# Transposes by upper and lower 64 rows into two PSUM banks, in a gated linear-attention and feed-forward kernel on one core

## The reference

```python
x = _layernorm(x + attn(x))     # attn(x) = x + y
x = _layernorm(x + ffn(x))
# attn: xn = layer_norm(x)*gamma+beta ; Q, K, V = xn @ W.T + b, 16 heads of 64 ; gate = silu(xn @ Wg.T + bg)
def step(h, qkv):
    h = alpha[None, :, :, None] * h + k[:, :, :, None] * v[:, :, None, :]
    o = jnp.einsum('bhi,bhij->bhj', q, h)
# y = (o * gate) @ WO.T + bO
# ffn: three cycles of out = out + coupling * twist(out), coupling from a four-layer net over out
#      (256, 128, 64, 1 wide, gelu, sigmoid) and from a small net over the mean of x
```

## Time and profile before

| | |
|---|---|
| median of 3 runs | 1892.21 us (1891.94 to 1892.32) |
| the profiled execution | 1892.58 us |
| its span | 1890.8 us |
| TensorE busy (matmuls) | 1824.6 us, 96% |
| VectorE, ScalarE, GpSimd busy | 56%, 37%, 17% |
| granted TensorE clock, mean | 0.985 of full speed |

### The profile page before, as it was taken

One profiled execution on the slowest core, in us unless ns is written; L12 is line 12 of the kernel. 1 busy time (PEld: TensorE's weight loads), 2 busy tenths in 40 slices (PEclk: granted clock), 3 DMA queues, 4 the chain that ended last, 5 costly groups with the idle time before them and its releaser, 6 DMA issues.

```text
span 1890.8 us, 43949 instructions
## 1 busy us (share of the span) xinstructions
PE 1824.6 (96%) x19120; PEld 1396.9 (74%) x19120; DVE 1062.4 (56%) x2214; ACT 699.9 (37%) x1282; POOL 312.9 (17%) x244
## 2 busy tenths in 40 slices
PE   5999999999899999999989999999989999999996
PEld 4888888863588888885368888888437888888732
DVE  7565555555745555554665645555565555555556
ACT  3323333344433333334433332323443333233344
POOL 4121211102212121110221112121022111212002
PEclk8999999999899999999989999999999999999998
DMA  4000000000100000000010000000001000000001
GB/s 161 2 13 2 13 2 12 2 1 1 56 2 13 2 12 2 12 2 1 0 57 2 13 2 13 2 13 2 1 1 57 2 13 2 13 2 2 2 0 45
DMA packets 22817, 26.11 MB, mean 14 GB/s; under 512 B 3169, under 2 KB 21473, under 8 KB 22625
## 3 DMA queue, kind: packets, MB, share of 16 engines
q1 hardware_dynamic: 20624, 19.09, 3.2%
q10 hardware_dynamic: 2000, 4.20, 0.6%
HBM read 14.90 MB, written 8.39 MB: 12 GB/s over the span
## 4 chain that ended last, share of the span: by engine, by line
PE 94%; DVE 3%; ACT 2%; POOL 1%; issue 0%; DMA 0%; ACTq 0%; DVEq 0%; SPq 0%
PE bank L848 39%; PE bank L923 12%; PE bank L1078 9%; PE bank L911 7%; PE bank L875 6%; PE bank L902 6%; PE bank L1095 4%; PE bank L892 3%; PE bank L884 3%; PE bank L1121 1%; PE bank L1108 1%; DVE stats L582 1%; PE bank L839 1%; DVE v_sb L816 1%; PE bank L934 1%; DVE x_nf L809 1%
## 5 line engine op out<-in xcount | busy, mean ns | idle before, releaser
L714 DVE TENSOR_TENSOR o_g<-bank,gate 128x512 f32<-128x512 f32 x128 | 88.6, 692 | 484.6 <-PE bank L911 484.6
L362 POOL TENSOR_TENSOR k_end<-k_sc,pows 128x512 f32<-128x512 f32 x128 | 134.9, 1054 | 1075.6 <-DVE k_sc L615 1075.6
L436 ACT ACTIVATE q_sb<-q_sb,pows 128x384 f32<-128x384 f32 (+2 forms) x384 | 167.3, 498 | 331.6 <-DVE q_sb L624 331.6
L454 ACT ACTIVATE h_bd<-h_seq,pows 64x256 f32<-64x256 f32 x256 | 129.9, 507 | 323.5 <-DVE h_seq L736 320.3
L923 PE MATMUL bank<-wo,o_g 128*128 128x256 f32 x1024 | 243.5, 380 | 0.8 <-DVE o_g L714 0.8
L923 PEld LDWEIGHTS bank<-wo,o_g 128*128 128x128 f32 x1024 | 192.7, 190 | 32.9 <-DVE o_g L714 1.0
L446 ACT ACTIVATE k_tok<-bank 128x512 f32<-128x512 f32 x128 | 76.5, 598 | 299.9 <-PE bank L884 299.9
L703 DVE COPY_PREDICATED att<-causal,bank 128x1024 f32<-128x1024 int32 x128 | 167.3, 1307 | 6.2 <-PE bank L875 5.4
L911 PE MATMUL bank<-att,v_sb 128*64 128x128 f32 x2048 | 140.1, 279 | 0.0
L902 PEld LDWEIGHTS bank<-q_sb,h_bd 128*128 128x128 f32 x1024 | 134.1, 191 | 7.4 <-ACT h_bd L454 0.2
L902 PE MATMUL bank<-q_sb,h_bd 128*128 128x128 f32 x1024 | 134.9, 275 | 0.0
(11 more groups left out here) (137 smaller groups left out, 3213.6 us busy)
## 6 DMA issues: line engine op xcount, KB each, us to landing
x_in<-in_x SPq DMA_DIRECT2D x16, 512.0 KB, 4.3
out_y<-q_sb SPq DMA_DIRECT2D x8, 512.0 KB, 2.8
out_y<-x_nf SPq DMA_DIRECT2D x8, 512.0 KB, 3.1
v_sb<-in_wq ACTq DMA_DIRECT2D x1, 1024.0 KB, 5.2
v_sb<-in_wk SPq DMA_DIRECT2D x1, 1024.0 KB, 9.0
x1t<-in_wg ACTq DMA_DIRECT2D x1, 1024.0 KB, 9.4
x1t<-in_wv ACTq DMA_DIRECT2D x1, 1024.0 KB, 13.5
wo<-in_wo ACTq DMA_DIRECT2D x1, 1024.0 KB, 17.4
```

Of the source, the lines that this page charges most:

```text
L362: nc.gpsimd.tensor_tensor(k_end[:].rearrange("p (a z) (b r) -> p a (z b) r", z=2, r=BL), k_sc[:].rearrange("p (a z) (b r) -> p a (z b) r", ...
L436: last = nc.scalar.activation(q_sb[:, p % 2, d].rearrange("p (a z) n -> p a (z n)", z=2)[:, :, reach], q_sb[:, p % 2, 0].rearrange("p (a z ...
L454: nc.scalar.activation(h_bd[rows, :, e * DH:(e + 1) * DH], h_seq[rows, :, :], ACT.Copy, scale=pows[rows, p, HP:HP + 1]).then_inc(s_hbd, 1)
```

## The change

Each 128 x 128 transpose becomes two of 64 rows by 128 columns. The upper 64 rows go into one bank and the lower 64 into the next, 64 columns each; what reads them picks the halves out of two banks. To have pairs of banks free, the bank plan of the attention changes: k and g always use bank 0, q bank 1, the updates bank 1, the transposed keys banks 0 and 1, the transposed input banks 2 and 3, and values go round banks 2 to 5. With this go changed waits on TensorE: the q projection waits for `s_hend`, the keys' transposes wait for the query and gate evacuations, and the transposes of the next step's input stand between g's projection and `y_part` at p = 6 instead of behind the keys. ScalarE scales the input's transposes ahead of `tokens_of` there.

```diff
-        def k_bank(p):
-            return p % 2
-        def q_bank(p):
-            return 1 - p % 2
         def g_bank(n):
-            return n % NP % 2 if n else 5
+            return 0 if n else 5
+        def halves_of(first_bank, first, count):
+            return psum[:, first_bank:first_bank + 2, first * DH:(first + count) * DH].rearrange(
+                "p r (c n) -> p c r n", n=DH)
+        def in_halves(rows):
+            return rows.rearrange("p (c r n) -> p c r n", r=2, n=DH)
...
         def final_rows(t, c):
-            return bank[(2, 0, 4, 6)[t] + c // 2][:, (c % 2) * D:(c % 2 + 1) * D]
+            first_bank = (2, 0, 4, 6)[t]
+            return psum[:, first_bank:first_bank + 2, c * P:(c + 1) * P]
         def v_bank(m):
-            return bank[(2, 3, 5, 1, 2, 3, 0, 5)[m]]
+            return bank[2 + m % 4]
...
-            def tokens_of(n, bk):
+            def tokens_of(n):
                 act.wait_ge(s_kt, n + 1 + C0)
                 act.wait_ge(s_upd, n + C0)
-                nc.scalar.activation(k_tok[:], part(bk, NC), ACT.Copy).then_inc(s_ktok, 1)
+                nc.scalar.activation(in_halves(k_tok[:].rearrange("p c m -> p (c m)")), halves_of(0, 0, NC),
+                                     ACT.Copy).then_inc(s_ktok, 1)
...
                             gate_of(p + 1, n + 1)
-                            tokens_of(n + 1, 4)
+                            if p == NP - 2 and following:
+                                x_scaled(it + 1)
+                            tokens_of(n + 1)
...
-            nc.vector.memset(bank[2], 0.0).then_inc(s_setv, 1)
-            nc.vector.memset(bank[3], 0.0).then_inc(s_setv, 1)
...
+            def by_halves(first_bank, place, src):
+                for e in range(2):
+                    rows = slice(e * DH, (e + 1) * DH)
+                    last = nc.tensor.transpose(bank[first_bank + e][:, place * DH:(place + 1) * DH],
+                                               src[rows, :], ident[rows, rows])
+                return last
...
-            def keys_transposed(bk):
+            def keys_transposed():
                 for c in range(NC):
-                    last = nc.tensor.transpose(bank[bk][:, c * C:(c + 1) * C], k_end[:, c, :], ident[:])
+                    last = by_halves(0, c, k_end[:, c, :])
...
                         if p + 1 < NP:
-                            pe.wait_ge(s_qev, n + 1 + C0)
-                            project("k", p + 1, k_bank(p + 1)).then_inc(s_k, 1)
-                            pe.wait_ge(s_gev, n + 1)
-                            project("q", p + 1, q_bank(p + 1)).then_inc(s_q, 1)
+                            project("k", p + 1, 0).then_inc(s_k, 1)
+                            pe.wait_ge(s_hend, n + 1 + C0)
+                            project("q", p + 1, 1).then_inc(s_q, 1)
                             pe.wait_ge(s_kev, n + 2 + C0)
-                            project("g", p + 1, g_bank(p + 1)).then_inc(s_g, 1)
+                            project("g", p + 1, g_bank(n + 1)).then_inc(s_g, 1)
+                        if p == NP - 2 and following:
+                            pe.wait_ge(s_xn, it + 2)
+                            pe.wait_ge(s_att, n + 1 + C0)
+                            x_transposed()
...
                         from_state(p)
                         if p + 1 < NP:
                             pe.wait_ge(s_kend, n + 2 + C0)
-                            pe.wait_ge(s_hend, n + 1 + C0)
-                            keys_transposed(4).then_inc(s_kt, 1)
+                            pe.wait_ge(s_qev, n + 2 + C0)
+                            pe.wait_ge(s_gev, n + 2)
+                            keys_transposed().then_inc(s_kt, 1)
...
                     if layer == 2:
                         for j in tiles:
                             if n == 0:
-                                pe.wait_ge(s_x1c, (b + 1) * NS * KT - 1 + j + C0)
+                                pe.wait_ge(s_x1c, (b + 1) * NS * KT + C0)
```

More of the change, by code:

```diff
@@ L412, in weight_high, with x_scaled, x_high @@
                 nc.scalar.activation(w_hi[w][:], w_in[n], ACT.Copy).then_inc(s_whi, 1)
-            def x_parts(step, banks_of):
+            def x_scaled(step):
+                act.wait_ge(s_xt, step + 1)
+                act.wait_ge(s_xlo, step + C0)
                 for k in range(KT):
[L417 to L420, removed]
+                    nc.scalar.activation(in_halves(x_f[:, k, :]), halves_of(2, k * NC, NC), ACT.Identity,
                                          bias=beta[:, k:k + 1], scale=gamma[:, k:k + 1]).then_inc(s_xf, 1)
+            def x_high(step):
                 act.wait_ge(s_xf, (step + 1) * KT)
@@ L459, in x1_copied @@
                 place = step % NS
+                act.wait_ge(s_x1t, step + 1 + C0)
                 for k in range(KT):
-                    act.wait_ge(s_x1t, step * KT + k + 1 + C0)
-                    nc.scalar.activation(x1t[:, k, place * ST:(place + 1) * ST], bank[first_bank + k],
-                                         ACT.Copy).then_inc(s_x1c, 1)
+                    nc.scalar.activation(in_halves(x1t[:, k, place * ST:(place + 1) * ST]),
+                                         halves_of(first_bank, k * NC, NC), ACT.Copy).then_inc(s_x1c, 1)
             def global_net(b, layer):
@@ L838, in x_transposed @@
                     for c in range(NC):
-                        last = nc.tensor.transpose(bank[k][:, c * C:(c + 1) * C],
-                                                   x_n[:, c, k * P:(k + 1) * P], ident[:])
-                    last.then_inc(s_xt, 1)
+                        last = by_halves(2, k * NC + c, x_n[:, c, k * P:(k + 1) * P])
+                last.then_inc(s_xt, 1)
             def products(dst, first, end, l_hi, l_lo, r_hi, r_lo):
@@ L892, in updates @@
                         last = nc.tensor.matmul(
-                            bank[4][e * DH:(e + 1) * DH, c * DH:(c + 1) * DH],
+                            bank[1][e * DH:(e + 1) * DH, c * DH:(c + 1) * DH],
                             k_tok[:, c, e * DH:(e + 1) * DH], v_sb[:, c, h * DH:(h + 1) * DH],
@@ L933, in x1_transposed @@
                     for c in range(NC):
-                        last = nc.tensor.transpose(bank[first_bank + k][:, c * C:(c + 1) * C],
-                                                   x_n[:, c, k * P:(k + 1) * P], ident[:])
-                    last.then_inc(s_x1t, 1)
+                        last = by_halves(first_bank, k * NC + c, x_n[:, c, k * P:(k + 1) * P])
+                last.then_inc(s_x1t, 1)
             def final_transposed(b, t):
@@ L942, in final_transposed @@
                     for k in range(KT):
-                        last = nc.tensor.transpose(final_rows(t, c)[:, k * P:(k + 1) * P],
-                                                   out_t[:, k, t * ST + c * C:t * ST + (c + 1) * C], ident[:])
+                        last = by_halves((2, 0, 4, 6)[t], c * KT + k,
+                                           out_t[:, k, t * ST + c * C:t * ST + (c + 1) * C])
                 last.then_inc(s_yt, 1)
@@ L949, in _ @@
             pe.wait_ge(s_xf, KT)
-            for n, (w, bk, done) in enumerate((("q", q_bank(0), s_q), ("k", k_bank(0), s_k), ("g", g_bank(0), s_g))):
+            for n, (w, bk, done) in enumerate((("q", 1, s_q), ("k", 0, s_k), ("g", g_bank(0), s_g))):
                 pe.wait_ge(s_wlo[n], 1)
@@ L1032, in _ @@
                             pe.wait_ge(s_qsh, n + 2 + C0)
+                            if p == NP - 2 and following:
+                                pe.wait_ge(s_xf, (it + 2) * KT)
                             scores(p + 1).then_inc(s_score, 1)
                     if following:
[L1036 removed]
+                        pe.wait_ge(s_hend, (it + 1) * NP + C0)
+                        project("q", 0, 1).then_inc(s_q, 1)
                         pe.wait_ge(s_kev, (it + 1) * NP + 1 + C0)
```

53 lines of the change are left out of this document (21 added, 32 removed).

## The result

| | before | after |
|---|---|---|
| median of 4 runs each | 1892.08 us | 1911.57 us (1910.89 to 1912.76) |
| ratio to before, 95% interval | | 1.0104 (1.009 to 1.0117): slower |
| the profiled execution, its span | 1892.58, 1890.8 us | 1912.76, 1911.0 us |
| granted TensorE clock, mean | 0.985 | 0.985 |

The change costs 19.5 us, or 1.0% (1911.57 less 1892.08), and 20.2 us in the two profiled executions. The prediction was 1907.0 in a range from 1899 to 1921. In the kernel after, `project` is L862, `y_part` L937, `from_state` L916, `from_chunk` L925, the updates L906, the scores L889, and all transposes are L846.

A forecast was written before the change was run, and what follows sets the result against it. TensorE, with 94% of the chain that ended last, was taken to bound the kernel. -5.8 + 2.2 - 1.0 + 2.1 + 17.3 = +14.8 us gave 1907.0 us against the median of 1892.21; range 1899 to 1921.

The forecast's parts named there:

- The two waits at p = 0: Each step's first pair: q waits for the carried state, keys for gate; gaps of 0.8 and 0.7 us, together +17.3 us.
- the 0.06 + 0.11 + 0.23 of the prediction: At p = 0, from state carried (324.43) to q's load (324.49), then 0.11 and 0.23 to q's second matmul (324.83).
- The first (no speed from halves): Rival: halves bring no speed, each pair costs 0.109 us; +52 us, 1944 us; chance 0.08.
- The second (k_tok): Rival: k_tok's copy out of two banks gets longer; +4 us, 1911 us, or 1921 with 0.2 more per copy; chance 0.11.
- The third (the waits don't bind): Rival: at p = 0 VectorE and ScalarE finish before TensorE comes; sum -8.3 us, 1884 us; chance 0.07.
- The fourth (no drain at a change of shape): Rival: changing into the 64*128 shape costs no additional drain; -14.2 us, 1893 us; chance 0.04.
- (a): Keys of head pairs 2 to 7, between from_state and from_chunk, 96 places: 0.465 us for 0.525, -5.8 us.
- (c): Transposes of the next input, moved between g's projection and y_part, 15 places: 0.81 us for 0.87, -1.0 us.
- The delay at p = 0 inside a batch: Waits for state and gate make from_chunk's load 0.91 us later in 12 steps with x1 behind the keys, 10.9 us.
- (b): Keys between two value projections, 16 places: 0.575 us for 0.436, +2.2 us.
- (d): x1 of each batch's last step, 4 places: layer 2 must wait for both copies, +0.52 us each, +2.1 us.
- The first steps of batches 2 to 4: A table load stands before gate; updates, which already wait for k_tok, come +1.7 us later each, +5.1 us.

The follow-up runs named there:

- e2: The kernel after, with VectorE masking pair 0 behind its state updates as for the other pairs; 1894.33 us, ratio 1.0011 to the kernel before.
- e3: The kernel after, with g of pairs 1 to 7 in a bank of its own, bank 4; 1896.82 us, ratio 1.0025 to the kernel before.
- e4: The kernel after with both pair 0's masks behind the state updates and g in bank 4; 1881.73 us, ratio 0.9945 to the kernel before.
- e1: The kernel after, bank plan and waits kept, but each transpose whole, 128 x 128; 1921.57 us, ratio 1.0155 to the kernel before.
- e9: e4 with each step's first keys transposed behind the eighth value projection and not the sixth; 1878.24 us, ratio 0.993 to the kernel before.
- e5: The kernel before, with only pair 0's masks put behind its state updates; 1894.72 us, ratio 1.0014 to the kernel before.
- e6: e4 with whole transposes in place of halves; 1892.84 us, ratio 1.0004 to the kernel before.
- e10: e9 with each step's first keys as four whole transposes, all others still halves; 1878.83 us, ratio 0.9932 to the kernel before.

## Why the prediction was right, point by point

**Right, mechanism and place.** The two waits at p = 0 are there in all 16 steps, 0.70 and 0.65 us where 0.8 and 0.7 were forecast, and name the state update and gate. The q projection's second matmul follows the end of the state update (326.73) by 0.40 us, which is the 0.06 + 0.11 + 0.23 of the prediction. e2, e3 and e4 show the cause: without the two waits, the 19.5 us turn into -10.4. The pairs 1 to 6 have no gap, k_tok's copy out of two banks lasts 599 ns where it was 598, and pairs of halves are 0.06 us apart.

**The rivals.** The first (no speed from halves) fell by e1. It was also what the load rule of the Trainium skill would have given ("TensorE: Matmul & The Clock Gate", section "LDWEIGHTS (loading the stationary operand)"). The trace does not agree: the halves' loads, 128 columns each, are recorded at 137 ns, where the rule makes 107 of it, and in x1's halves a new one starts every 0.03 us. The second (k_tok) fell by the 599 ns. The third (the waits don't bind) fell by the 16 + 16 waits; its -8.3 us is near the -10.4 of e4, where they are taken away. The fourth (no drain at a change of shape) fell too: in e4 the step boundary gained 0.22 us when one change of shape was saved (e9), and (a) gained 0.04 and not 0.15.

**The sizes.** The sum was 5.4 us too low against the profiled execution. By the terms of the prediction:

- (a) and (c), -6.8, measured -5.1, or about -4.2 without the four places where g's projection was held up before. A pair's keys gain 0.04 us and not 0.06: from the first load to `from_chunk`'s it is 0.40 us (341.68 to 342.08), where a load and three pairs at 0.058, the last stream of 0.054 and one drain of 0.09 were to give 0.376. The second pair is what is late, 0.11 us behind the first and not 0.058. Edit (c) was mis-sized too: the distance that has it with the keys gains 0.07 and not 0.12.
- The delay at p = 0 inside a batch, with (b): 1.05, measured 1.18. Two things add up in the fourth step: the keys load 0.11 us and not 0.06 behind gate's end (331.24 to 331.35), and the 12 pairs of halves take 0.92 us to `from_chunk`'s load and not 0.84. This gives +1.6.
- (d), +0.52, measured +0.49: from the start of x1's first copy to layer 2 it is now 1.14 us (411.97 to 413.11), where the earlier trace rows have 0.65. The change of shape ahead of these halves, which the prediction left out here, lets them begin 0.1 us later: 12.61 us behind the last pair's `from_chunk` and not 12.51.
- The first steps of batches 2 to 4: the relief, since k_tok is no longer waited for, was expected at all three and came at one. At the two others TensorE's granted clock fell, +1.4 us each (last section).
- The start: -1.05 us that I had not foreseen, also a matter of the clock. No run ties it to the change.
- One stretch of scores that took 1.38 us for 1.00, +0.4. Why is open. It is not in e1, e2, e3 or e4 at that place.

So no step of the argument failed; the mis-sized ones are the halves (by 1.7 us, and by 2.6 without the four places), the step boundary (by 1.6) and the clock, which was not in the sum. The clock's two parts, +2.7 and -1.05, and the four places partly cancel; that they leave the measured time so near the forecast is luck.

## What to carry to other kernels

A bank plan is a plan of waits. When two uses share a bank, look up the order in which the engine that empties it does its work, at every place of the loop and not only in the steady state. Here pairs 1 to 6 had 0.4 us to spare, and the first pair of each step, with one `masked` ahead of the state update, cost more than all the halves saved.

When such a wait bites, look for both ends: free the bank (g in bank 4) and let the releasing engine do the wanted work first (the masks behind). Transposes of a smaller tile shape pay where a neighbour on TensorE changes the shape anyway: in front of the scores the halves gain 0.04 us for a pair's keys, between two value projections they lose 0.14.

## What the runs showed of the hardware that was not expected

**TensorE at half clock behind a gap of 2 us.** At the first step of batches 2 to 4 a table load makes the second wait 2.06 us long. At two of these three places the clock then fell. The timeline of the second batch's first step shows the work behind the gap drawn out, and the windows (window, its us; busy time and count of PE, PEld, DVE, ACT, POOL; the granted clock; DMA share and GB/s) what was granted:

```profile
520.71 0.47 PE L846 MATMUL bank<-ident,k_end 64*128 64x64 f32 x8 [2.06 <-ACT gate L432]
521.10 1.60 PE L925 MATMUL bank<-att,v_sb 128*64 128x128 f32 x16
...
522.48 1.07 PE L906 MATMUL bank<-v_sb,k_tok 128*64 128x64 f32 x16
...
523.49 1.51 PE L889 MATMUL bank<-q_sb,k_sc 64*32 64x128 f32 x64
```

```profile
518.00:521.00 3.00, 0.94 (x14) 0.78 (x13) 0.00 (x0) 2.53 (x4) 0.00 (x0) 1.00 0.00 0
521.00:525.00 4.00, 4.00 (x103) 3.65 (x98) 1.92 (x6) 1.01 (x2) 0.00 (x0) 0.57 0.01 4
1460.00:1463.60 3.60, 3.60 (x93) 3.32 (x90) 2.18 (x7) 1.02 (x3) 0.00 (x0) 0.53 0.02 5
```

The third row is the same place in the fourth batch. `from_chunk` took 1.60 us for 1.09, the updates 1.07 for 0.63, the scores 1.51 for 1.00: a granted 0.57 over 4.00 us is some 3.4 us at the lower level, 1.2 GHz, and 1.4 us were lost. At the third batch's first step, with the same gap of 2.06 us, nothing of the kind happened (`from_chunk` 1.09, scores 1.00), nor at any of the three places in e1, whose gaps are 2.05 to 2.07. Behind the gaps of 1.6 us at these places in e2 it didn't happen either. So such a gap can cost its length and 1.4 us more, and did so at two of six places. What decides it these runs don't show.

**The clock at the start.** Both kernels begin their first 36 value matmuls at almost the same time, and the chain of work that ended last gives them different lengths, first before, then after:

```profile
29.78 11.34 PE bank L848 x36
```

```profile
29.66 10.29 PE bank L862 x36
```

In both the early ones last 0.63 us, as at half clock, and later ones 0.39. The step up comes at about 35.7 us before and 33.4 after. The granted clock from 33.4 to 35.5 is 0.50 before and 0.99 after. This is the 1.05 us of the start. It goes with no edit: with whole transposes e1 has 0.50 in that window, e5 0.79 and e6 0.92, and with halves e4 has 0.80 and e10 0.91. So up to about 1 us of any comparison of two profiled executions here can be the moment of this step.
